# Dense cross attention in a decoder: within a key tile, both accumulations into the output move ahead of the second score product, and the by-query products stand in one run

## The reference

```python
q = (xn @ w_q).reshape(B, SQ, 16, 64)
k, v = jnp.split(context @ w_kv, 2, axis=-1)
scores = jnp.einsum('bqhd,bkhd->bhqk', q * 64 ** -0.5, k)
attn = jax.nn.softmax(scores, axis=-1)
out = jnp.einsum('bhqk,bkhd->bqhd', attn, v).reshape(B, SQ, 1024)
```

## Time and profile before

| | us |
|---|---|
| time before, median of 3 runs | 8585.87 (8582.94 to 8592.92) |
| the profiled execution, its own time | 8577.81 |
| its span | 8576.0 |
| the stage `attend_wide` with heads in both layouts, from first to last by-key product | about 6931 to 8407 |

### The profile page before, as it was taken

How to read it: one execution, slowest core, us unless ns; L and a number is a source line. 1 busy time by engine, 2 the same in 40 slices (tenths; PEclk the granted TensorE clock), 3 DMA queues, 4 the chain that set the end, 5 groups by cost and what they waited for, 6 DMA issues and landing times. The chain is left out here.

```text
span 8576.0 us, 157847 instructions
## 1 busy us (share of the span) xinstructions
PE 6475.1 (76%) x31084; PEld 2656.0 (31%) x31210; DVE 6513.2 (76%) x41686; ACT 4446.3 (52%) x8495; POOL 4015.2 (47%) x2691
## 2 busy tenths in 40 slices
PE   6998476775677667999575777776747889999995
PEld 2333122222222224565222222222212422222223
DVE  4664799999999995555699999999998354444443
ACT  1665466664566653111576777776747423333331
POOL 0001355553455542222365666665646046666662
PEclk7999666666666666999677777776767999999997
DMA  2000000000000000000100000000000411111111
GB/s 76 19 22 9 34 8 5 8 5 5 8 5 8 5 5 17 15 22 7 41 5 9 6 9 6 9 6 5 9 5 2 156 43 29 41 30 31 30 39 45
DMA packets 79239, 180.51 MB, mean 21 GB/s; under 512 B 22160, under 2 KB 36494, under 8 KB 76686
## 3 DMA queue, kind: packets, MB, share of 16 engines
q1 hardware_dynamic: 73098, 161.58, 6.5%
q10 hardware_dynamic: 5124, 8.39, 0.4%
HBM read 110.58 MB, written 58.57 MB: 20 GB/s over the span
## 5 line engine op out<-in xcount | busy, mean ns | idle before, releaser
L2170 DVE TENSOR_REDUCE l1xc_part_max<-l1xc_by_query 128x1 f32<-128x512 f32 (+1 forms) x1024 | 559.0, 570 | 681.3 <-PE l1xc_by_query L2029 657.7
L2130 ACT ACTIVATE l1xc_prob<-l1xc_less_max 128x512 f32<-128x512 f32 (+1 forms) x832 | 451.4, 594 | 990.3 <-PE l1xc_less_max L2043 990.3
L582 PE MATMUL l1ac_by_query<-l1ac_k_stack,l1ac_q_stack 97*128 (+1 forms) x1024 | 421.7, 469 | 700.2 <-ACT keep_xT L677 363.8
L552 POOL TENSOR_SCALAR l1ac_lost<-l1ac_score,l1ac_tops 128x2048 bf16<-128x2048 f32 x128 | 696.0, 5437 | 411.3 <-DVE l1ac_tops L789 399.8
L770 DVE MAX8 l1ac_cand<-l1ac_score 128x8 f32<-128x39 f32 (+1 forms) x6656 | 863.2, 192 | 31.7 <-ACT l1ac_score L677 16.9
L582 PE MATMUL l0xc_by_query<-l0xc_k_stack,l0xc_q_stack 97*128 (+2 forms) x1024 | 378.1, 434 | 666.2 <-ACT keep_xT L677 449.4
L770 DVE MAX8 l1ac_cand<-keep_xT 128x8 f32<-128x39 f32 (+1 forms) x6656 | 863.0, 191 | 4.4
L1982 POOL TENSOR_TENSOR l1xc_total<-l1xc_total,l1xc_prob 128x2048 f32<-128x2048 f32 (+1 forms) x176 | 794.1, 4512 | 72.4 <-POOL l1xc_v_tile L1997 72.3
L770 DVE MAX8 l0xc_cand<-l0xc_score 128x8 f32<-128x31 f32 (+1 forms) x6656 | 800.3, 182 | 27.9 <-ACT l0xc_score L677 15.8
L552 POOL TENSOR_SCALAR l1ac_lost<-keep_xT,l1ac_tops 128x2048 bf16<-128x2048 f32 x128 | 696.3, 5440 | 243.8 <-DVE l1ac_tops L789 243.8
L770 DVE MAX8 l0xc_cand<-keep_xT 128x8 f32<-128x31 f32 (+1 forms) x6656 | 801.0, 181 | 4.4
(11 more groups left out here) (484 smaller groups left out, 14388.2 us busy)
## 6 DMA issues: line engine op xcount, KB each, us to landing
l1xc_k<-wide_k SPq DMA_DIRECT2D x32, 400.2 KB
moe_w<-in_L_ffn_mlp_w_dram SPq DMA_DIRECT2D x16, 512.0 KB, 4.1
wide_q<-l1xp_full SPq DMA_DIRECT2D x8, 1024.0 KB, 3.9
wide_q_parts<-l1xp_parts SPq DMA_DIRECT2D x16, 512.0 KB, 5.5
l1xc_q_hm<-wide_q_parts SPq DMA_DIRECT2D x32, 256.0 KB, 3.8
l1xc_q<-wide_q SPq DMA_DIRECT2D x32, 256.0 KB
wide_sums<-l1xc_o_out ACTq DMA_DIRECT2D x64, 128.0 KB, 2.3
wide_k<-l1xp_full SPq DMA_DIRECT2D x8, 800.5 KB, 3.4
```

What stands on the lines that cost most here:

```text
L552: nc.gpsimd.tensor_scalar(lost[:, i % 8, 0:nk], score[i % 4][:, 0:nk], tops[:, i % 8, TOPK - 1:TOPK], None, ALU.is_lt).then_inc(masked, 1)
L582: nc.tensor.matmul(sA[c % 2][:, 0:w], Qm[0:SHIFT_ROW, bass.ds(at + i * P, P)], Kb[0:SHIFT_ROW, bass.ds(at + a, w)], start=True, stop=True) ...
L2130: nc.scalar.activation(prob[0:n, buf(j), c], yP[c % 2][0:n], ACT.Exp).then_inc(y_taken, 1)
L2170: nc.vector.tensor_reduce(part_max[:, i % 2, c:c + 1], a_bank(i, c)[:, 0:w], AX.X, ALU.max).then_inc(a_taken, 1)
```

## The change

Within a key tile PE's stream was: first `by_key`, two jobs by query, `sums` (p = 0), one job, second `by_key`, two jobs, `sums` (p = 1), the remaining job. It becomes: first `by_key`, both `sums`, second `by_key`, and then all jobs of the tile without a break. The instructions are the same in number and size; the streams of DVE, ACT, POOL and SP are unchanged.

```diff
@@ in attend_wide, PE's head(ha, hb, slot), the loop over the key tiles @@
                     todo = jobs_of(j) if ha is not None else []
                     if j == NKT - 2 and ha is not None:
                         a_end(ha)
+                    by_key(hb, slot, j, 0)
                     for p in range(2):
-                        by_key(hb, slot, j, p)
-                        for i, c in (todo[0:2], todo[3:5])[p]:
-                            by_query(ha, 1 - slot, i, c)
                         if j:
                             sums(hb, j - 1, p)
                         elif not first:
                             sums(hb - 1, NKT - 1, p)
-                        for i, c in (todo[2:3], todo[5:])[p]:
-                            by_query(ha, 1 - slot, i, c)
+                    by_key(hb, slot, j, 1)
+                    for i, c in todo:
+                        by_query(ha, 1 - slot, i, c)
                     if j < 2 and not first:
                         denominators(hb - 1, j)
```

## The result

The changed kernel takes 8759.05 us (median of 4 runs, 8754.57 to 8762.69), the kernel before on the same occasion 8584.41 us. The ratio is 1.0203, with a 95% interval of 1.0191 to 1.0216: slower by 2.0%, or 175 us. It lies within the forecast range of 8645 to 8785, but 49 us above the forecast of 8710.

A forecast was written before the change was run, and what follows sets the result against it. PE's own work was taken to bound the stage. Losses of 136, 18, 13, 7 and 1 less a gain of 71 gave +104 us; with +20 for the clock, 124, a median of about 8710 us, range 8645 to 8785.

The forecast's parts named there:

- What bounds the stage: In a 1093 us stretch of the stage PE is busy 97% and sets the pace; DVE, ACT and POOL do not.
- The gain, -71 us: Tiles with jobs: fewer leavings of a job group (0.10 us each) and adjacent `sums` (0.15) save 71 us over 15 heads.
- The dearer drains of the rival: Rival: each of four switches between product kinds costs 0.15 us, giving +79 before the clock, 8665; chance 9%.
- Loss 1: Runs of jobs in a tile outpace DVE's reductions over three banks: 0.89 us waiting per six-job run, +136 us.
- The 130 us announced as waits: Sign: the profile after shows PE waiting for `part_max` some 130 us, in pieces of 0.1 to 0.6.
- Loss 2: Turning of the maxima after tile 10's run: PE idles 1.7 us instead of 0.5 in 15 heads, +18 us.
- Loss 3: Tiles without jobs wait for ACT's exponentials: +13 us in tiles 11 and 12, +7 last head, +1 first tile.
- Sum without the clock: Whole stage: 136 + 18 + 13 + 7 + 1 - 71 = +104 us.
- Loss 4: New idle stretches of 1.7 us at 15 heads' turnings lower PE's clock: between 0 and 54 us, taken as +20.
- The rival by which the clock falls as a rule: Rival: every turning or head's end costs a full slow-clock spell of 8.5 us, 128 on top of 104, 8818; chance 12%.
- a stage clock well under 0.95: Sign that the forecast was wrong: the stage's granted clock after the change lies well under 0.95.
- the DVE run: Rival: DVE's whole run of reductions lies on the path, 0.45 us more a tile, +70, 8760 without the clock; chance 7%.

The follow-up runs named there:

- e9: Kernel before, with single jobs behind each `sums` moved ahead of it and the turning of the maxima behind tile 11's first score product: 8528.88 us, ratio 0.9938.
- e3: Changed kernel, with the turning of the maxima behind tile 11's first score product and tiles without jobs in the old order: 8647.33 us, ratio 1.0071.
- e6: Changed kernel, with three jobs moved ahead of the adjacent `sums`, the turning covered and tiles without jobs in the old order: 8538.77 us, ratio 0.9953.
- e5: Changed kernel, with DVE reducing only the first 64 columns of each bank, the rest of the maximum left out: 8580.32 us, ratio 0.9993.
- e4: Changed kernel, with products of zeros run in the gaps at the turning and in tiles 11 and 12, except in the last head: 8687.82 us, ratio 1.0128.
- e2: Changed kernel, with tiles without jobs put back in the old order (score product, sums, score product, sums): 8720.12 us, ratio 1.0162.
- e1: Changed kernel, with the turning of the maxima moved behind the first score product of tile 11: 8715.04 us, ratio 1.0151.

## Why the prediction was right, and where it was mis-sized

- **What bounds the stage.** Right: DVE, ACT and POOL worked as much as before, and the stage's 178 us stand in PE's order, its waits and its clock.
- **The gain, -71 us.** Confirmed in the tiles: the one of e9 gives 0.11 for a leaving, where 0.10 was taken, and two `sums` side by side take 1.87. The sums of whole runs support it more loosely: e3 gives 136 - 71 = 65 as 68, e6 44 for 46 with 12 us of clock in it, e9 55 for 38. The dearer drains of the rival (0.15 for every switch) did not appear: the changed tile took 7.86, not 7.73. That the 0.10 and 0.15 are drains at all, no run here shows.
- **Loss 1, +136 us for the runs.** Confirmed: the cadence stands in the rows, and without DVE's long reductions (e5) a tile is 0.79 to 0.85 us shorter. The 130 us announced as waits in the profile were 79.8; the loss is right and the announced row was not, since the profile counts a drained matmul as busy.
- **Loss 2, +18 us at the turning.** 1.62 us of idle for 1.7; in all 24.3 after 7.3, 17 us more.
- **Loss 3, +21 us for the exponentials.** Tile 12 took 5.78 us from `by_key` to `by_key` (7759.18 to 7764.96), where 5.77 were worked out, and tile 11, where the clock stays up, 5.86 for 5.87. One thing was seen otherwise: at the starts of the rounds the idle time without a releaser nearly vanished (11.3 us in 6 pieces to 4.7 in 2), since the wait for ACT now lies over it.
- **Sum without the clock, +104 us.** e4, which keeps every wait and restores the clock, stands 108 us above the kernel before. Its clock is even a little better (20 us at 1.2 GHz for 38), so that the order and its waits cost up to 9 us more than that.
- **Loss 4, the clock, taken as +20: this is the term that was mis-sized.** It is 71 us by e4 and 67 to 70 by the granted clock. Two steps failed. First, the gap at the turning was priced below the middle of 0 to 54 because the first head's run idles and keeps 1.00; alone it costs some 50 (e2 against e3), near the upper bound. There the idle time comes in pieces of 0.2 us, here in one of 1.6: the nearest row in length was the better guide. Second, the two gaps of 1.2 us in tiles 11 and 12, which loss 3 itself works out, were left out of the clock's term without a reason; they add some 20 on top, and alone they cost nearly as much as the turning (e1 against e3). With 71 for 20 the sum is 8584 + 104 + 71 = 8759. A reading was off as well: the window of the earlier trace rows holds five of the six starts of a round, not six, and 19 us of lost clock (38 us at 1.2 GHz) rather than 22; this changes the bound little.
- **The rival by which the clock falls as a rule** was nearer in its mechanism than the forecast, which gave it 12%: the clock did fall in nearly every head, at some 5 us a head instead of 8.5. The sign "a stage clock well under 0.95" was just missed, at 0.95. That the time lies in the range is owed to the range's width on that side, which was made for the DVE run and half of the clock's way.

The behaviour that the Trainium skill describes ("TensorE: Matmul & The Clock Gate", A second HAM failure mode: psum-queue depth-cycling), short idle times between groups that make the clock swing, was set aside on the evidence of the first head's run. Inside the runs this case's traces still do not show it: e3 has every pause of the runs and a clock of 0.99. At the head's end, behind single gaps of 1.2 to 1.6 us, the clock did swing; the one at the turning is not a wait for a bank.

## What to carry to other kernels

Here a run of products into three banks was free up to three (e6, e9); from the fourth on it ran at the pace of the engine that empties the banks, although that engine is idle half of the time overall. Expect the same of other counts, but only three was measured. Before grouping like work, ask what each moved piece was covering: here the `sums` covered reductions, exponentials and the turning of the maxima at once, and e9 shows that the saving from fewer switches could be had without giving up any of that. Price a new gap on TensorE not only by its length but by the work behind it that then runs at 1.2 GHz, count every new gap, and do not simply add the prices of neighbours. And hold a total that fits against its tiles: three totals here (e5, e6 and the rival's 8760) fitted in part by chance.

## What the runs showed of the hardware

- Adding 1.7 us (at the turning) and 1.07 us (in tiles 11 and 12) of useless products to the gaps made the kernel 71 us faster (e4): the waits stayed, and the granted clock of the stage went from 0.95 to 0.99. The lengths 1.7 and 1.07 are estimates, made before the run from the number of products.
- Three gaps of 1.62, 1.17 and 1.16 us, within 16 us, brought TensorE to 1.2 GHz behind the first and the last in the head that is shown; filling one kind gave 49 or 59 us, filling both 71. Against e3, the first alone cost 48 us in 15 heads and the others alone 45, by the time at 1.2 GHz.
- Four float32 products of `sums` followed by four of the same shape last 0.86 us from start to start, followed by another shape 1.01; from `sums` to `denominators` it is 0.91.
- A wait for a bank that cost 0.89 us in a run of six jobs was shown as 0.36 us of idle time.
